# The last group's triangle product in 32x32 array tiles, and its k transposed by TensorE

## The reference

```
zn = sparse_norm(gn(x))                       # one mean and variance over everything
a  = sigmoid(zn @ W_ga.T + b_ga) * (zn @ W_la.T + b_la)
b  = sigmoid(zn @ W_gb.T + b_gb) * (zn @ W_lb.T + b_lb)
k  = einsum('bitc,bjtc->bijc', a, b)          # per sequence and channel, 32 x 32 by 32 x 32
kn = sparse_norm(k)                           # mean and variance of the WHOLE k
x  = x + sigmoid(zn @ W_go.T + b_go) * (kn @ W_lo.T + b_lo)
```

## Time and profile before

| what | us |
|---|---|
| median of 3 runs | 345.86 |
| lowest and highest | 344.46, 346.84 |
| the profiled execution's own time | 347.44 |
| its span in the profile | 345.5 |

### The profile page before, as it was taken

The page is one execution under the profiler, slowest core; times in us unless marked ns, Lnnn a source line. Parts: engine busy times, 40 slices in busy tenths (PEclk is TensorE's granted clock), DMA queues, the critical chain, the costliest instruction groups (busy, mean ns, idle before and its releaser), DMA issues.

```text
span 345.5 us, 7455 instructions
## 1 busy us (share of the span) xinstructions
PE 249.6 (72%) x2982; PEld 151.5 (44%) x2982; DVE 258.1 (75%) x466; ACT 217.3 (63%) x392; POOL 195.8 (57%) x169
## 2 busy tenths in 40 slices
PE   0056965599779779679679669769864599998724
PEld 0046342377347346346346347346531145554223
DVE  4985789766797898898898895899796764431972
ACT  4635787389569669669579669468341447567512
POOL 6890564659885896886877843434840862000620
PEclk9995799658998999999999998998997599999856
DMA  7100122013031031031031022100000014667207
GB/s 248 31 0 30 33 63 63 0 39 86 0 93 32 2 92 35 1 93 32 5 88 34 30 64 55 40 0 3 2 2 0 1 30 93 169 183 199 62 0 243
DMA packets 34893, 19.66 MB, mean 57 GB/s; under 512 B 21228, under 2 KB 31788, under 8 KB 34860
## 3 DMA queue, kind: packets, MB, share of 16 engines
q1 hardware_dynamic: 34860, 19.20, 20.7%
HBM read 8.71 MB, written 6.29 MB: 43 GB/s over the span
## 4 chain that ended last, share of the span: by engine, by line
DVE 41%; PE 36%; ACT 14%; issue 7%; DMA 1%; POOL 1%; DVEq 0%; ACTq 0%
PE PS L1126 31%; DVE t_sb L876 6%; DVE nmax L892 5%; DVE S_sb L896 4%; DVE og L869 4%; DVE gn_part L964 3%; DVE sums L820 3%; ACT u_sb L593 2%; ACT PP L623 2%; DVE Z L1113 2%; DVE Z L1117 2%; PE PS L1390 2%; ACT t_sb L607 2%; PE PS L1195 1%; DVE st L830 1%
## 5 line engine op out<-in xcount | busy, mean ns | idle before, releaser
L1126 PE MATMUL PS<-znT,A_bd 128*128 128x512 f16 x192 | 46.9, 387 | 11.8 <-DVE t_sb L876 10.5
L427 POOL TENSOR_TENSOR S_sb<-S_sb,rden 128x512 f32<-128x512 f32 x32 | 35.5, 1133 | 27.7 <-DVE rden L838 27.7
L876 DVE TENSOR_TENSOR t_sb<-PS,t_sb 128x512 f16<-128x512 f32 x64 | 41.1, 683 | 8.6 <-ACT t_sb L607 8.6
L607 ACT CAST t_sb<-PS 128x512 f16<-128x512 f32 x64 | 36.6, 611 | 15.0 <-PE PS L1126 13.5
L613 ACT ACTIVATE S_sb<-S_sb 128x512 f32<-128x512 f32 x32 | 20.2, 631 | 31.8 <-DVE S_sb L896 31.8
L1126 PE MATMUL PS<-zbd,t_sb 128*128 128x64 f16 x768 | 28.9, 199 | 13.6 <-DVE t_sb L876 12.8
L433 POOL TENSOR_TENSOR PP<-S_sb,PP 128x512 f16<-128x512 f32 x28 | 31.8, 1158 | 12.0 <-ACT PP L601 12.0
L1126 PEld LDWEIGHTS PS<-zbd,t_sb 128*128 128x128 f16 x768 | 26.0, 102 | 25.1 <-DVE t_sb L876 16.7
L1126 PE MATMUL PS<-PP,Z 128*128 128x128 f16 x512 | 34.6, 236 | 0.2 <-DVE PP L850 0.2
L593 ACT COPY u_sb<-PS 128x512 f32<-128x512 f32 x64 | 33.7, 626 | 1.6 <-PE PS L1126 1.4
L1126 PEld LDWEIGHTS PS<-znT,A_bd 128*128 128x128 f16 x192 | 16.9, 99 | 40.6 <-DVE t_sb L876 23.9
(11 more groups left out here) (198 smaller groups left out, 529.5 us busy)
## 6 DMA issues: line engine op xcount, KB each, us to landing
Z<-zn_dram SPq DMA_DIRECT2D x64, 64.0 KB, 2.8
x_tok<-in_x SPq DMA_DIRECT2D x4, 512.0 KB, 5.6
zn_dram<-zn_tok SPq DMA_DIRECT2D x8, 256.0 KB, 2.0
zbd<-znT SPq DMA_DIRECT2D x32, 64.0 KB, 2.0
k_dram<-og SPq DMA_DIRECT2D x4, 512.0 KB, 3.6
th<-k_dram SPq DMA_DIRECT2D x16, 128.0 KB, 2.7
out_x<-u_sb SPq DMA_DIRECT2D x4, 512.0 KB, 3.3
PP<-u_sb SPq DMA_DIRECT2D x8, 128.0 KB, 2.4
```

The costliest lines, as they stand in the source:

```text
L427: nc.gpsimd.tensor_tensor(P, P, bcast(rden[:, 32 * k:32 * k + 32], 2, N), ALU.mult).then_inc(p_nrm, 1)
L607: nc.scalar.copy(t_sb[:, HI, :, h], bank_tg(h)[:, :].rearrange("p (q i) -> p q i", i=N)).then_inc(t_hi, 1)
L876: nc.vector.tensor_tensor(t_sb[:, LO, :, h], bank_tg(h)[:, :].rearrange("p (q i) -> p q i", i=N), t_sb[:, HI, :, h], ALU.subtract).then_in ...
L1126: return nc.tensor.matmul(o, l, r, start=start, stop=stop)
```

## The change

The group g = 3 is treated in another way; groups 0 to 2 stay.

- `bbd_load(3)`, `k_store(3)` and `k_load(3)` are taken out of SyncE's queue.
- `triangle_last` takes b straight from `b_buf[1]`: for each channel c and each sequence n one product of 32 partitions with 32 columns by 32 columns, in the tile of the array that belongs to partitions 32n of input and output: 128 matmuls in place of 32. It puts out (position, channel, position) with the sequence on the partition groups, all four of a bank's partition groups being written by different tiles.
- It stands behind gate unit 1 and no longer behind gate unit 5. Gate units 2 to 5, eight transposes (`transpose_last`), the sums' two matmuls and gate units 6 and 7 follow.
- On ScalarE `k_copies(3)` stands behind gate unit 1; it writes k with the channel innermost, so that consecutive elements of the bank go to places 32 elements apart.
- VectorE copies the transposed k from two banks into `kT`, after the small steps and before the output units (semaphore `k3_ok`). `lo` of units 4 and 1, whose banks held the transposes, and of 6 and 7, which read that kT, wait for it.

```diff
+        k_last = k_sb[:, 1024:2048]
...
             bbd_load(2)
             k_store(sp, 1)
             k_load(sp, 1)
-            bbd_load(3)
             k_store(sp, 2)
             k_load(sp, 2)
-            k_store(sp, 3)
-            k_load(sp, 3)
...
                     dst = k_sb.rearrange("p (s c m) -> p s c m", s=2, c=8)[:, g % 2, 4 * h:4 * h + 4]
-                    nc.scalar.activation(dst.rearrange("p c m -> p (c m)"), PS[3 + i % 4][:, :], ACT.Identity,
+                    if g < 3:
+                        dst, src = dst.rearrange("p c m -> p (c m)"), PS[3 + i % 4][:, :]
+                    else:
+                        act.wait_ge(k_sq, i - 1)
+                        dst = k_last.rearrange("p (i c) -> p c i", c=D)[:, 16 * h:16 * h + 16]
+                        src = PS[3 + i % 4][:, :].rearrange("p (c i) -> p c i", c=16)
+                    nc.scalar.activation(dst, src, ACT.Identity,
                                          accum_out=ksum[:, 0, i:i + 1]).then_inc(k_cp, 1)
...
-            out_gates(range(0, 6))
+            out_gates(range(0, 2))
             k_copies(3)
-            out_gates((6, 7))
+            out_gates(range(2, A4))
...
             dve.wait_ge(go_th, 8)
+            for h in range(2):
+                dve.wait_ge(k3_mm, h + 1)
+                nc.vector.tensor_copy(kT.rearrange("p (f m) -> p f m", f=A4)[:, 4 * h:4 * h + 4, 384:512],
+                                      PS[3 + h][:, :].rearrange("p (f m) -> p f m", f=4)).then_inc(k3_ok, 1)
...
-            out_gates(range(0, 6))
-            triangle(3)
-            out_gates((6,))
+
+            def triangle_last():
+                pe.wait_ge(pj_ok, 64)
+                for h in range(2):
+                    pe.wait_ge(k_sq, h + 3)
+                    for c in range(16 * h, 16 * h + 16):
+                        for n in range(4):
+                            rows = slice(L * n, L * n + L)
+                            last = mm(PS[5 + h][rows, L * (c % 16):L * (c % 16) + L], b_buf[1][rows, c], a_buf[1][rows, c])
+                    last.then_inc(k_mm, 1)
+
+            def transpose_last():
+                pe.wait_ge(k_cp, 8)
+                pe.wait_ge(k_sq, 6)
+                for f in range(A4):
+                    last = nc.tensor.transpose(PS[3 + f // 4][:, 128 * (f % 4):128 * (f % 4) + 128],
+                                               k_last[:, 128 * f:128 * f + 128], ident[:, :])
+                    if f % 4 == 3:
+                        last.then_inc(k3_mm, 1)
+
+            out_gates(range(0, 2))
+            triangle_last()
+            out_gates(range(2, 6))
+            transpose_last()
             pe.wait_ge(k_ok, 1)
             mm(PS[7][:, 0:2], allsum[:, 1], ksum2[:, :]).then_inc(ks_mm, 1)
-            out_gates((7,))
+            out_gates((6, 7))
...
-                                     (4, k_sq, 8), (1, k_sq, 8), (3, k_sq, 8), (5, k_sq, 8),
+                                     (4, k3_ok, 1), (1, k3_ok, 2), (3, k_sq, 8), (5, k_sq, 8),
                                      (6, lo_s, 1), (7, lo_s, 2)):
                 pe.wait_ge(engine_sem, n)
-                pe.wait_ge(kT_ld[u // 2], 64)
+                if u < 6:
+                    pe.wait_ge(kT_ld[u // 2], 64)
+                else:
+                    pe.wait_ge(k3_ok, 2)
                 lo(u)
```

More of the change, by code:

```diff
@@ L243, in build @@
         k_st = [sem("k_st0"), sem("k_st1")]
-        kT_ld = [sem(f"kT_ld{g}") for g in range(4)]
+        kT_ld = [sem(f"kT_ld{g}") for g in range(3)]
         go_mm = sem("go_mm")
@@ L248, in build @@
         ks_mm = sem("ks_mm")
+        k3_mm = sem("k3_mm")
+        k3_ok = sem("k3_ok")
         lo_mm = sem("lo_mm")
```

## The result

| | this kernel | the kernel before, beside it |
|---|---|---|
| median, us | 350.01 (4 runs) | 345.49 (4 runs) |
| lowest and highest | 349.44, 351.90 | 344.46, 346.84 |
| ratio, 95% interval | 1.0139 (1.0096 to 1.0182) | |
| profiled execution: own time, span | 350.4, 348.4 | 347.44, 345.5 |

The change makes the kernel 1.4% slower. 345.3 was forecast (0.6 us less than before), with a range to 347.6: the prediction is wrong in sign and in size.

The account below looks back on a forecast made before the run. Bound: the chain through VectorE's unbroken 14.05 us to the last transposes. Sums' matmuls 0.98 us earlier, but VectorE's copies (1.25, mostly in an idle hole) leave its first unit at 319.5 against 320.14: -0.6, 345.3 us; range 343.6 to 347.6.

Parts of the forecast that it names:

- The bound: Last 40 us: the end moves with VectorE's first output unit at 320.14; the last k's DMA wait has 3.8 us slack.
- I take 64 rounds of four at 0.029, 1.9 us: TensorE's last triangle product: 256 records, four tiles at once, 1.9 us in all; bounds 1.8 to 7.4 us.
- The prediction's own sign of being wrong: Late TensorE queue: wrong if the sums' matmuls come before 315 or after 317, or VectorE's stretch changes by over 1 us.
- The copies' size, 0.60 us: ScalarE's evictions of the last k, written at steps of 128 bytes: 0.60 us each as now, with 1.07 possible.
- rival B: ScalarE's strided evictions take 1.07 us each instead of 0.60: +0.94 us, 346.3 in all; chance 0.18.
- VectorE's row: Evidence for unslowed ScalarE evictions: VectorE's projection products write float pairs at 128-byte steps in 0.283 us, dense copy 0.288.
- Rival A: Last triangle product: small tiles writing one bank don't run side by side, 7.4 us, +4.6, 350.5 in all; chance 0.10.
- TensorE's queue: Gate unit 5 and eight transposes stand before the sums' matmuls, ending 315.94, 0.98 earlier; the queue eats 1.8 us.
- VectorE: Before the output units: two new copies, 1.25 us, first unit at about 319.5 instead of 320.14; its 14.05 us stay.
- The final transposes: At the kernel's end, after VectorE's last addition: 6.03 us stay; half a microsecond either way belongs to the forecast.
- C: Final transposes all at the faster clock: 3.7 us, 2.4 less, 342.9 in all; chance in full 0.03.
- the unforeseen: Anywhere in the kernel: something no forecast or rival names, in either direction; chance 0.07.

Follow-up runs that it names:

- a2: The changed kernel with the last triangle product made for every second channel only, 128 records instead of 256; 348.86 us in one run.
- after: The changed kernel itself, as profiled, against the kernel before; median 350.01 us, ratio 1.0139.
- a4: The changed kernel with TensorE writing the channel innermost into the bank, so ScalarE writes k in runs of 16 floats; 351.36 us, ratio 1.0153 to the kernel before.
- b4: The changed kernel with product spread among gate units, dense write of k, split evictions, transposes and sums' matmuls earlier, copies in gaps; 346.43 us, ratio 1.0016 to kernel before.
- b2: The kernel before with a burst of 256 extra small f16 matmuls put in at 264 us, results unused; 344.61 us in one run.
- a1: The changed kernel with SyncE's store of group 2 of k waiting until the last triangle product is done; 349.00 us, ratio 1.0099 to the kernel before.
- b1: The changed kernel with the last product cut into four parts of 64 records, a gate unit ahead of the first three; 347.77 us in one run.
- c1: The kernel before with GpSimd's four additions given to VectorE, which does all eight; 346.23 us, ratio 1.0021.

## Why the prediction was wrong

**The bound.** Right. The end moved with VectorE's first unit: 3.94 us later counted from gate unit 0, 3.99 at the end. The DMA wait that the change removed was worth nothing, as said.

**"I take 64 rounds of four at 0.029, 1.9 us": here it failed.** The step put the supply of instructions at nothing, without a row for it. Its other terms held: the start was right (1.40 after gate unit 0, forecast 1.41), and so was the rate: 150 records start within 1.28 us, 0.0086 apart against the 0.0073 taken. But the last record starts 7.3 us after gate unit 0 and not at about 3.3, because 3.13 us of hole lie inside the product and the rest of it runs slower. The step treated the price of a record as all that a record costs. No row was asked how fast TensorE can be given instructions, though the change turned 128 instructions into 512 in the same time, and 256 of them, which lasted 3.9 us at the rate of the triangle product before (64 records in 1.95 us), now last 1.1. With 3.1 to 3.6 us from crossing to new instructions the one is covered, the other not. The queue that brings them, with 23 packets, stood in the page of the kernel before, unread.

The Trainium skill's "Runtime: NRT & Kernel Launch", Instruction fetch mechanics, says that instructions are fetched in blocks of 16 KiB, 256 instructions, the next while the current one runs, and that the crossing is mostly hidden. On the blocks the trace agrees (16384 bytes a packet). That the crossing is hidden holds only for slow instructions; where 256 instructions ran in 1.1 us, it cost 2.2 to 3.1 us.

**What it did down the chain.** ScalarE's second eviction was forecast 3.85 us after gate unit 0 and came at 7.58. In a2, without the hole, it comes at 4.15. So 3.43 of it is the hole, 0.30 the slower first copy. From the tanh of unit 2 to the transposes it took 2.09 us instead of a2's 1.47: when that tanh began (316.25) TensorE was still at gate unit 3, slowed by clock 0.50 up to 316.8. That is 0.62 more. Their sum, 4.05, is the difference between a2's first unit and after's (11.75 and 15.82, 4.07). The prediction's own sign of being wrong came: the sums' matmuls start 12.0 us after gate unit 0, 320.3 on its scale of time, where it allowed 317. The other 0.5 of the miss of 4.58 is in a2 as well:

**The copies' size, 0.60 us.** Wrong, and rival B right in mechanism: 1.03 us. On the path it came to 0.6 at the tanh of unit 2 and 0.5 at VectorE's first unit (a2), and not to the 0.94 of the rival, since a copy and its square together went from 1.15 only to 1.47 (a4, after): the square starts before the copy has ended. The Trainium skill's "SBUF — State Buffer", in the section on Door 1, puts a penalty on each access that enters a new 16-byte line. ScalarE's single floats at steps of 128 bytes agree (1.03 us), as do the runs of 64 bytes that cost nothing (0.60, a4). VectorE's row, which I had preferred as nearest, wrote pairs, by another engine.

**Rival A.** 350.5 was its time and 350.01 was measured, but it didn't happen. Four row groups wrote into one bank 0.0086 us apart; one after the other it would have been 0.029, by the prediction's estimate from the earlier trace rows. The rule that the prediction named beside it, the Trainium skill's "TensorEngine Tiling (Array Packing)", Gotcha 1, isn't borne out here for tiles that write different partitions of the bank. That the two times agree is an accident.

**TensorE's queue.** Right: gate unit 5 waited for ScalarE's tanh, and the transposes stood in front of the sums. In a2 unit 5 starts 0.81 after the tanh of unit 2 (0.76 forecast), the sums' matmuls end 8.22 after gate unit 0 (7.68, and 0.5 for the copies).

**VectorE.** Right: two copies in 1.29 us, the first unit 3.53 after the sums' matmuls in a2 (3.56 forecast), the stretch 14.05 us.

**The final transposes.** 5.5 us instead of 6.0, within the forecast's half microsecond; C did not come.

**The chances.** Every rival was a price of an engine. 0.07 for the unforeseen was too little for a form that no row showed, 256 records of it in a row.

## What to carry to other kernels

Before cutting matmuls finer, count instructions and not only columns: a matmul with its weight load is two, and here 256 of them had to last 3.1 to 3.6 us (4.4 behind a large transfer), at 3.5 us 0.027 us for each matmul with its load; below that TensorE ran dry however well the tiles overlapped. A stall called "issue" that stays at the same instruction count and moves when instructions are added far ahead is one of supply; long matmuls set between short ones took it away but for 0.3 us (b4). And a transfer or wait that is off the path is worth nothing, however much work its removal saves.

## What was not expected of the hardware

- TensorE runs dry in a burst: 300 instructions in 1.28 us and then 3.1 us of nothing in f32 32x32 tiles (after), 442 in 1.8 us and then 2.3 us of nothing in f16 128x32 tiles (b2).
- A store of 512 KB delays the packet of instructions by up to 1.2 us more (after against a1), so a transfer that no engine waits for can hold TensorE.
- The hole is paid twice: in after the granted clock is 0.50 from 313.50 to 316.80, behind it, and in each other kernel with a hole of over 2 us at this place the clock falls too; in b1 and b4 it doesn't.
- TensorE's 32x32 tiles write PSUM with a step of 16 floats at the same rate as densely: 150 records in 1.47 us either way (a4).
- VectorE's addition takes 2.19 us beside GpSimd's (before) and 1.02 alone (c1).
